# The last batch of a decoder layer by halves of its queries, with a replanned order of steps

## The reference

```python
x = x + attn(layernorm(x))            # causal, 16 heads of 16, scale 0.25
x = x + xattn(layernorm(x), ctx)      # keys and values from ctx, (4, 77, 256)
x = x + ffn(layernorm(x))
# ffn(x): scale = sigmoid(clip) * max|x| / 127, over the whole of x
#   xq = clip(round(x / scale), -128, 127) * scale; weights likewise, by row
#   h = quant(silu(xq @ wg.T) * (xq @ wu.T)), scale again from max over all of h
#   return h @ wd.T
```

## Time and profile before

| what | value |
|---|---|
| median of the runs | 1051.85 us (3 runs, 1050.81 to 1053.42) |
| the profiled execution | 1059.1 us, span of its trace 1057.4 us |
| TensorE (PE) busy | 905.4 us, 86% |
| VectorE (DVE) busy | 716.3 us, 68% |
| ScalarE (ACT) busy | 611.8 us, 58% |
| GpSimd (POOL) busy | 363.6 us, 34% |
| mean granted TensorE clock | 0.925 |

### The profile page before, as it was taken

One profiled execution on the slowest core, in us unless ns is written; L12 is line 12 of the kernel. 1 busy time (PEld: TensorE's weight loads), 2 busy tenths in 40 slices (PEclk: granted clock), 3 DMA queues, 4 the chain that ended last, 5 costly groups with the idle time before them and its releaser, 6 DMA issues. The chain is left out here.

```text
span 1057.4 us, 16929 instructions
## 1 busy us (share of the span) xinstructions
PE 905.4 (86%) x5859; PEld 449.9 (43%) x5863; DVE 716.3 (68%) x1413; ACT 611.8 (58%) x1114; POOL 363.6 (34%) x377
## 2 busy tenths in 40 slices
PE   2889999799899999999998989999997478667656
PEld 1534344264435443644453436444353334433234
DVE  7688776567677838677678286777714874379764
ACT  1426775545576576456766654567864145247594
POOL 7821343242421065333201652243112320047424
PEclk9979999999999999999999999999998776769877
DMA  4320123820221411112204111122006021021026
GB/s 151 114 79 26 46 65 68 113 65 34 91 75 32 159 38 56 46 61 75 83 30 160 41 58 39 61 80 81 25 22 196 6 79 40 40 100 60 1 80 199
DMA packets 79723, 75.97 MB, mean 72 GB/s; under 512 B 18984, under 2 KB 73896, under 8 KB 79640
## 3 DMA queue, kind: packets, MB, share of 16 engines
q1 hardware_dynamic: 74632, 71.36, 22.0%
q10 hardware_dynamic: 3456, 2.94, 0.9%
q0 software_dynamic: 1552, 0.58, 0.6%
HBM read 22.43 MB, written 13.13 MB: 34 GB/s over the span
## 5 line engine op out<-in xcount | busy, mean ns | idle before, releaser
L672 ACT ACTIVATE probs<-psum 128x512 f32<-128x512 f32 (+1 forms) x608 | 311.9, 577 | 183.1 <-PE psum L862 180.7
L1027 DVE CUSTOM_DVE_ANT_0 junk<-psum,mask 128x640 bf16<-128x640 f32 (+3 forms) x256 | 252.9, 1022 | 56.6 <-PE psum L827 54.8
L592 POOL TENSOR_SCALAR_AFFINE_SELECT probs<-probs 128x512 f32<-128x512 f32 x128 | 81.8, 642 | 391.3 <-ACT probs L672 391.1
L862 PE MATMUL psum<-q_stack,k_stack 98*128 98x512 bf16 (+3 forms) x768 | 185.5, 332 | 8.7 <-DMA q_stack<-max_rows 4.2
L887 PE MATMUL psum<-probs,v_sb 128*17 128x512 f32 (+3 forms) x1536 | 157.5, 491 | 3.0 <-POOL probs L592 2.7
L1023 DVE TENSOR_REDUCE rowmax<-psum 128x4 f32<-128x512 f32 (+2 forms) x96 | 97.5, 1045 | 78.0 <-PE psum L821 77.3
L827 PE MATMUL psum<-k_stack,q_stack 96*128 96x512 bf16 (+3 forms) x512 | 128.8, 346 | 5.5 <-DVE rowmax L1027 3.6
L862 PEld LDWEIGHTS psum<-q_stack,k_stack 98*128 98x128 bf16 x768 | 62.8, 98 | 137.6 <-ACT probs L672 80.9
L787 PE MATMUL psum<-xnT,wT 128*128 128x512 f32 x192 | 93.9, 628 | 0.3 <-ACT xprobs L677 0.3
L714 PE MATMUL psum<-wT,xnT 128*128 128x256 f32 x384 | 88.0, 388 | 0.2 <-DVE rowmax L1023 0.2
L714 PEld LDWEIGHTS psum<-wT,xnT 128*128 128x128 f32 x384 | 74.1, 196 | 11.1 <-issue 0.8
(11 more groups left out here) (155 smaller groups left out, 1264.4 us busy)
## 6 DMA issues: line engine op xcount, KB each, us to landing
q_stack<-q_parts SPq DMA_DIRECT2D x192, 64.0 KB, 2.6
k_stack<-k_parts SPq DMA_DIRECT2D x192, 64.0 KB, 2.6
xq_stack<-xq_parts SPq DMA_DIRECT2D x192, 64.0 KB, 2.6
xn<-in_x SPq DMA_DIRECT2D x8, 512.0 KB, 5.5
res<-in_x SPq DMA_DIRECT2D x4, 1024.0 KB, 9.2
resid_hbm<-res SPq DMA_DIRECT2D x8, 512.0 KB, 2.6
resid<-resid_hbm SPq DMA_DIRECT2D x8, 512.0 KB, 4.7
out<-o_sb SPq DMA_DIRECT2D x8, 512.0 KB, 3.2
```

Of the source, the lines that this page charges most:

```text
L592: nc.gpsimd.affine_select(out=tile, in_=tile, compare_op=ALU.is_ge, fill=0.0, base=0, pattern=[[0, GH], [1, P]], channel_multiplier=-1).th ...
L672: nc.scalar.activation(probs[n % 2][:, heads * k:heads * k + heads, 0:cols], bank_a(s)[:, 0:heads * cols].rearrange("p (h n) -> p h n", h= ...
L862: last = nc.tensor.matmul(bank[:, cols * n:cols * n + cols], k_stack[:, slot, h, P * j:P * j + P], q_stack[:, slot, half, h, q0 - HALF * h ...
L1027: nc.vector.tensor_tensor_reduce(out=junk[D_STEPS.place(s) % 2][:, 0:keys], in0=bank_d(s)[:, 0:keys], in1=m.mask[:, T - keys:T], scale=1.0 ...
```

## The change

`parts` gives the last batch by halves: half 0 and half 1 are visits, holds, layernorms and cross-attention pieces of their own. Batch 3 then has eight holds instead of four (20 in all). A hold of half 1 loads the keys of both halves, so four k stacks of half 0 (24 DMAs) are added. So are eight trips of maxima (`mT`, `shift`), four `yN`, four `xyN`, a second `rstd` in each of the two layernorms behind batch 3's attentions, a second bias of the cross-attention and a second `xmax`. The matmuls of scores, values and projections, and the exponentials, are the same in number. The list of 1915 picks becomes one of 1947, and all of it is new, from the first steps on. `feed_forward` is not touched.

```diff
@@ -93,7 +93,7 @@
 def parts(b):
-    return (BOTH,)
+    return (0, 1) if b == B - 1 else (BOTH,)
@@ -254,25 +254,25 @@
 PICKS = (
-    "pppppppkppppppppvkkpkppppppqqpppmqmmmmmkmmqmmmmmmqqmsssmsmsmsssmvmssmvsmmvvmkmpvmmmpppvsssqmsmpmkkssqmsp"
...
-    "vvvvxxxxxrxxxxwxxxxxxxxwcwxxwwwxxwwwwccwwwcccccccxcccwwdddcdxddcdddcdwwwcdddddcccwddccddcdcwddccddcddccc"
-    "ddcdddcddcddddwddddddwdxxxxxxxxxxxxxxxxxxxx")
+    "prppppppkpqpppppppvqpppppqmmmmmmpmqmmmmmmmmkqmmmssmssqmpsqssmsvmmsvmsskmmmmmvrvvmmppssqqsvsssmmvmsssmmsm"
...
+    "srxxssxxssvssssvssssxxvsxxvssxvvvvyywyccccyccyyxddyyccddyycwcdywwwwwdddcddcwcccwwdddddcccdcccdccddddcccd"
+    "ydcdddcddxxwdcwwwwxdcdddccdxcdcdwccwwdddwccdccwxxxxddddddxxdwdxyywyyyyyyyyy")
```

More of the change, by code:

```diff
@@ L272 @@
-    "mcdddvcvmdscscvsssmvdvsqqssdssmddvscmmddvsmssmvscsvcsssmvmmsdddvccmdccsdmssmdssmmssvssmsddddmsvssmdmssvs"
-    "sdvmmdscddccdvvvcssdccsssdsssvddddvssdddvsddvssvdssvdsssvxxxxxsssxxssvssxxsvsssxssvsxsssvxssxxxxxvrsxxxx"
-    "vvvvxxxxxrxxxxwxxxxxxxxwcwxxwwwxxwwwwccwwwcccccccxcccwwdddcdxddcdddcdwwwcdddddcccwddccddcdcwddccddcddccc"
-    "ddcdddcddcddddwddddddwdxxxxxxxxxxxxxxxxxxxx")
+    "prppppppkpqpppppppvqpppppqmmmmmmpmqmmmmmmmmkqmmmssmssqmpsqssmsvmmsvmsskmmmmmvrvvmmppssqqsvsssmmvmsssmmsm"
@@ new lines @@
+    "ssmvmsssmmvmmsqsmsssmvsmsssmvmssvsqmmmmkvvvssspksvpsspsksvmpssmvsqmvsmssskmvsmqvpppsmmvssmmsssmvmsssmsms"
+    "vmsssmqsmvssmsmsvsmspvspqmmmpmvvvmsssmsvssmssvssqmvsmvssmsvvsmsmpmmspmmssvssmmssvssqmkmssvsmssqmsvssmsms"
+    "vssvsqmmpmmvvvmssmssmsvsssmqvsspvsmmpmvssmmsvvssmpmmssvsqsmmssvssmmssvskkksmmsssvsmsssmvqssvmmmsqmmpmmvv"
+    "vqmsssvssvvsssmvmssmvmxmsxmvsmssmxxmvsmsvskkkxxxssvsssmmsvsmssxvssmmsssvssmssvsmmkqqxsvsqkqmmvxxxxvvsssv"
+    "sxmssxxvsssmxmsxxmvsmxmmvsssmmsvvmsssmvmcssmssmvsscccssscccvssccmmcxcccsddcdcdxccmdddmmqddvsmssdcvsmmcss"
@@ new lines @@
+    "dddccddcscdqvsccdmcmdddmvssmmssvvdcsscssdddvqcddmvsccsddvqcsmdmddvmssmdsmsvssmvcddddmvdmssmdddmmddvmssmd"
+    "msssdssmvxsmxxxvmmssxsssxxxxxxsssvsxsvsvssvvssssxxxvsxxxxrsvssxxvspppvsspppssvvrsssvsssssvsssvssssspvpss"
+    "ssvssxppvspppqppvvqqvpvvvmmmqpqqmmmpmmmmmmmmpmmpmmmmmmxxxmmmmmxmsmssqqmssxxsmssvmssmvmsmvsmssmvsvmsssmvm"
+    "smsssvxssmmssvsmsssmsvsmsssqqvsmmsvsqqxxcmmxxvvvxxssssvssmssvxxxxvmssmxsmxmmxmmqvssmsvmsvsmssmvssmmssvcs"
+    "cmsssvcssccscssvscmsmcscxsccdcdmddmxmdcdcdddvvqmcmmccsssmmdvvvsdddcsdvsdccssmdssmmdddvsdcsscdvvqqcccssmd"
@@ new lines @@
+    "sscsvmdddcccdvsscdvcdmdmddmssmdssmcddddmvdmssmdddmmddvssmmssdmsssdsvsxmscxxxvmmsxxsssxxvsvsxxxxxxxrsssvs"
+    "vxsssvvssvsxxxxxvssssvvsssspprpppvssssvssssvssssvssssvssppvspxppvvvpppppvqpppvvqqmpmmpmmmmmqmmxmxxmxsmsm"
+    "sssxsssvsmmsxxxvxxxsvxqsssxvvsssssvvssqvsqxxxvxxxmvmqmvxmmmmmmmmmssvssmssmssvsmmsvscccvvvcssccsssccscxvs"
+    "scvcccddcxcqqqdmmdvmcsssmmmdmdmdddmmvvvqqmdmmddddmdmmddmmqmdddmvmmssmssmssmsvmsssmsmsvssmcmssvssmmssvsss"
+    "mmsvssvsmcccvccvvdmscccvqsscsscsscdsdvsssqqmmsvmsmsssmvssmmssvsmdmsssmvmssdmvscdcddccmdmddvmvqqvqdmddddv"
@@ L277 @@
+    "dmmmmdmdddmmdsmssmdmssmcssdsmvmxxmxxmsxxxxxsssvssmmssvsmsssvsmmxxxxxsssvssvsvsxvrxvxxxxxxvsssssssvssxxvs"
+    "srxxssxxssvssssvssssxxvsxxvssxvvvvyywyccccyccyyxddyyccddyycwcdywwwwwdddcddcwcccwwdddddcccdcccdccddddcccd"
+    "ydcdddcddxxwdcwwwwxdcdddccdxcdcdwccwwdddwccdccwxxxxddddddxxdwdxyywyyyyyyyyy")
 ORDER = order_of(PICKS)
```

## The result

The changed kernel is slower. Its median is 1063.04 us (1054.61 to 1067.86, 14 runs) against 1053.01 us for the kernel before (1047.32 to 1056.22, 14 runs) on the same chip: ratio 1.0084, 95% interval 1.0057 to 1.0111. The forecast was 1039 us with a range of 1021 to 1058: sign and size are both wrong. Of the rivals' numbers, that of (c), 1067.7, is the nearest.

What follows compares the result with a forecast made beforehand. TensorE was taken to bound the stretch from 80 to 790 us, but not the last batch's tail. Terms -29.5 + 13 - 8.6 + 7.9 + 5 = -12.2 us gave 1039 us, range 1021 to 1058.

Steps and rivals of the forecast that it cites:

- (c): Rival: the ring of short visits runs dry, three uncovered turns lose 33 instead of 5 us, 1067.7 us; chance 0.15.
- Term 1: Front of the tail, last self-attention transposes to first cross-attention scores: 43.5 to 14 us, gain 29.5.
- Term 2: Body of the tail, the cross-attention pieces: 59 to 72 us from work moved into it, cost 13, bounds 59 to 84.
- rival (b): Gain given back in the body, 84 instead of 72 us, as weight rounding delays score maxima; 1051.6 us, chance 0.13.
- Term 3: End chain of transposes, projection and layernorm, with four tiles instead of eight: 23.2 to 14.6 us, gain 8.6.
- Term 4: Front work of half 0 moved ahead of the last `pv`, where TensorE is full: cost 7.9 us, bounds 6 and 12.
- Term 5: Short visits of batch 3's self-attention, round trips partly uncovered by other steps: cost 5 us, bounds 0 and 33.
- Replanning: Rest of the list in a new order with the same work: 0 us, bounds -6 and +6.
- The base: Whole kernel before: median 1051.85 us, 7.3 below the profiled 1059.1, so the forecast 1046.9 becomes 1039.6.
- the self-attention end: Sign for the cost ahead of the tail: self-attention ends 8 to 15 us later than 806.

Runs made afterwards that it cites:

- self_halves: Only the last batch's self-attention by halves, in the new order; whole-batch tail in the old order. 1064.04 us, ratio 1.0124 to the kernel before.
- early_replan: The kernel before, without halves, with its first 930 steps in the new order and the rest in the old: 1050.26 us, ratio 0.9980.
- cross_halves: The kernel before with its old order and whole self-attention visits; only the tail behind them goes by halves: 1061.14 us, ratio 1.0097.
- late_maxima: The changed kernel with one to four more TensorE steps ahead of `mT` in seven of batch 3's eight visits: 1070.55 us, ratio 1.0161 to before.
- early_light: early_replan with the row maxima of batch 3 taken over the first 128 keys only: 1047.09 us, ratio 0.9932 to the kernel before.
- early_store: early_replan with batch 2's projections, layernorms, cross-attention steps and stores up to 30 picks earlier: 1095.55 us, ratio 1.0406 to the kernel before.

## Why the prediction was wrong

Point by point, with the terms of the prediction:

- **Term 1, front 43.5 to 14:** measured 11.4 in the trace. The mechanism was right: the scores waited for the six copies on SP behind the weight loads (4.35 us of wait, DMA engines 0.99 busy in the window); the time is just under the lower bound of 12. But self_halves has a front of 34.3 us with the tail of before, and no wait for the store in it: its self-attention ends later, when the stores have landed. Against the 40.9 of early_replan, 6.6 us of the front go by being late alone, and they are no gain that the halves of the tail bring.
- **Term 2, body 59 to 72:** measured 76, inside 59 to 84, 4 us too small. Against before (57.8) it is 18.2 us: 7.7 of work at full clock (forecast 9.7), 5.1 more idle, 5.4 more at the lower clock. The 3 us "for the queues" should have been 10. TensorE's waits in the body for the split maxima went from 3.2 to 5.0 us and those for their copy into the stack from 1.0 to 4.1 us, while the one for rounded weights, on which rival (b) rested, was 7.5 us in the tail of before and is 2.5 in the body now.
- **Term 3, end chain, gain 8.6:** measured 24.7 to 16.0 by the table's bounds, gain 8.7. Right to its parts (wait 6.76 where 6.9 was worked out).
- **Term 4, work moved ahead, 7.9:** self_halves to the kernel after is 6.5 us (822.9 to 829.4), of which 6.3 is work at full clock (730.8 to 737.1). Right.
- **Term 5, short visits, 5 us:** measured 22.5 in self_halves against early_replan. **This is the step that failed.** The bound, 3 turns x 11 = 33, held, and rival (c) set the point of decision at 17 us; the choice near the lower end was wrong. I chose it because the new list puts 6 to 9 us of filler into each turn. The filler is there, but steps are taken in order: what stands behind `mT` doesn't fill a wait at `mT`, and in two of the four short visits of half 0 nothing stands ahead of it. Putting some there brought 7.5 us more, with waits in other places. Two things were not in the term at all: the lower clock (6.0 us), and 4.2 us of matmul time, 3.4 of them for the same matmuls. Nor was it the stack copies, with which the term's round trip begins and on which rival (c) rests, that TensorE waited for: 0.8 us for a k stack in self_halves, against 7.8 for the maxima. These waits at the maxima matmuls are the sign that the prediction gave for (c).
- **Replanning, 0 ± 6:** early_replan is -0.2% (-0.5 to +0.1%). Right for the first 930 steps, which is what it has of the new list.
- **The base:** taking -7.3 us from the profiled time of before to its median was right for before. It hides that about 5 of them lie ahead of the tail, and so the self-attention end of the kernel after is 28 us later than the 801 of the two other traces, not 23.2 as against 806. The forecast was 8 to 15.

The sum of what was measured, in the traces: +23.2 ahead of the tail, -32.1 front, +18.2 body, -8.7 end chain, +0.2 the rest, that is +0.8 us (1057.4 to 1058.1 with rounding). The medians say +10.0. The rest is in which executions were profiled: that of before lies 6.1 us above its median, of which 4.5 are ahead of the tail (806.2 against 801.7 in cross_halves), and that of after 3.2 below its own: 0.8 + 6.1 + 3.2 = 10.1. So against a usual execution of before the first term is nearer to +28 than to +23.

Put into the prediction's own sum, term 5 at 22.5 turns -12.2 into +5.3 and so settles the sign; term 2 at 18.2 makes it +10.5, and the other three as measured +6.4. The experiments give the same in another cut: self-attention by halves costs 13.8 us by the medians (early_replan to self_halves), and the front of half 0 moved ahead together with the halves of the tail then gives back 1.0 (self_halves to the kernel after). In the traces that tail is 113.1 us against 103.4, and 6.5 of the 9.7 us are paid ahead of it. So with the halved self-attention taken as given, the rest of the change brings nearly nothing.

Of rival (c), shown is that half-size visits, in this list's order, cost 22.5 us ahead of the tail in the traces (13.8 us of the whole by the medians; the unchanged tail behind them is 12 us shorter, 6.6 of it in the front), that it is not the replanned order of the first 930 steps, that the copies' issue and traffic are a few us of it by the medians, or nothing, and that about a quarter is VectorE's reductions. That the idle part of the rest is the uncovered round trip of the maxima is argued from the waits and from where `mT` stands; late_maxima, which should have shown it, came out slower. How the 12 us of idle time divide among the waits for `negmax`, POOL's mask and the stacks was not tried one by one, and a list with filler ahead of every `mT`, planned for it, was not tried either.

The clock. The prediction weighed a sentence of the Trainium skill, "TensorE: Matmul & The Clock Gate" (Part 1, the HAM clock gate), that for modelling the ramp penalty is under 1% of a typical span; it stands there beside the warm-up at a kernel's start. By the granted clock of the records, the time lost to the lower clock is 55.0 us in the kernel before and 51.9 us in the kernel after, 5.2% and 4.9% of their spans, and the denser tail lost 20.7 us to it where the old one lost 23.6. The measurement decides: over the whole span it is five times the page's figure, since the lower level comes back again and again, in the tail and behind the two long waits above. Halving the visits moved it more (6.0 us in self_halves) than filling the tail saved (2.9).

None of the kernels with the reference's whole computation beats the one before by more than its interval. early_light is 0.7% faster with a shift of the softmax that is not the row's maximum in batch 3.

## What to carry to other kernels

Where one engine is busy 95% of the time and takes its steps in order, splitting a stage's pieces adds a round trip (maxima, transposes, copy back) for each extra piece. Count as cover only the steps that stand between the last one that feeds the waiting step and that step itself; two visits here had none (and adding some afterwards, in late_maxima, moved the waits and saved nothing). The cost can go on as a lower clock behind the wait. Size such a term from its uncovered end (here 22.5 of at most 33 us), or measure the split alone before planning the rest around it. And count a stage's filler once: in early_store, where the work of batch 2 was pulled forward, the self-attention of batch 3 ended 47 us later.

## What the hardware showed that I had not expected

- Time at the lower clock can be part of the cost of a wait: in self_halves the granted clock fell within two waits of 2.6 and 2.4 us and stayed at 0.50 for 6.8 and 10.2 us; behind the second, four 128x128 matmuls took 0.63 us instead of 0.39. Over the whole kernel the lower clock costs about 5% of the span.
- Executions of one program spread over 9 us of 1050, and the clock has a share in it: the same steps in the same order up to the tail ended at 806.2 and 801.7 us in two traces, with 17.0 and 11.1 us lost to the lower clock. One profiled execution each is not enough for differences of 5 us.
- The same 768 matmuls of the second pass took 3.4 us more at full clock in self_halves than in early_replan, by the records; why is open.
